# A two-layer graph network: the last h1 tiles, their Gram products and the channel statistics move ahead of the query heads

## The reference, cut to what matters

```
h   = relu(layernorm(x1))                       # "h1", 49 tiles of 128 rows
xn  = batchnorm(h)                              # mean and variance of each channel over all rows
agg = segment_sum(xn[src], dst) / max(deg, 1)   # 100,000 gathered rows
conv = relu(agg @ W_conv + b_conv)
# attention over the first 256 rows only (the batch is all zero, so one block of MAXN = 256)
qf, kf = phi(q, True), phi(k, False)            # random features, 256 of them, 8 heads of 64
attn = (qf @ (kf^T v)) / (qf @ sum(kf)) @ Wo
out = x1 + batchnorm(conv + attn + h)
```

## Time and profile before

| what | value |
|---|---|
| median of three runs | 3003.85 us |
| span of the profiled execution | 3541.0 us |
| the profiled execution's own time outside the span | not given by the page |
| mean granted TensorE clock | 0.883 of full speed |
| busy share: PE, PEld, DVE, ACT, POOL | 76%, 47%, 61%, 28%, 52% |
| gathers: first layer, second layer | 880, 784 |
| HBM traffic | 533.43 MB read, 54.10 MB written |

### The profile page before, as it was taken

One profiled execution on the slowest core, in us unless ns is written; L12 is line 12 of the kernel. 1 busy time (PEld: TensorE's weight loads), 2 busy tenths in 40 slices (PEclk: granted clock), 3 DMA queues, 4 the chain that ended last, 5 costly groups with the idle time before them and its releaser, 6 DMA issues. The chain is left out here.

```text
span 3541.0 us, 46052 instructions
## 1 busy us (share of the span) xinstructions
PE 2699.5 (76%) x10647; PEld 1671.1 (47%) x10692; DVE 2161.8 (61%) x3783; ACT 995.2 (28%) x3078; POOL 1858.0 (52%) x1883
## 2 busy tenths in 40 slices
PE   6887377777777877777777787877778788788991
PEld 4554256666656656655656652323333333233440
DVE  9999966666666767666668743333333333334668
ACT  6733334444443444434444520000000000000220
POOL 0000255555555556555555446666666666664667
PEclk8998678898988899898898897888889999999995
DMA  5110366666666666666665856666666666565226
GB/s 184 47 40 31 111 180 185 186 189 185 180 182 188 180 191 189 183 192 176 177 189 191 288 152 174 176 180 178 178 176 178 173 173 175 171 174 157 67 66 251
DMA packets 243449, 588.25 MB, mean 166 GB/s; under 512 B 57744, under 2 KB 82832, under 8 KB 243400
## 3 DMA queue, kind: packets, MB, share of 16 engines
q0 software_dynamic: 133120, 443.52, 43.8%
q1 hardware_dynamic: 110280, 144.14, 12.4%
HBM read 533.43 MB, written 54.10 MB: 166 GB/s over the span
## 5 line engine op out<-in xcount | busy, mean ns | idle before, releaser
L506 POOL DMA_INDIRECT big<-feat_table,idx x880 | 841.3, 956 | 1020.8 <-ACT idx L531 407.5
L1133 POOL DMA_INDIRECT big<-h_table,idx x784 | 743.6, 948 | 460.6 <-issue 235.2
L801 PE MATMUL psA<-big,onehot 128*128 128x260 f32 x1760 | 504.0, 436 | 120.1 <-DVE big L683 95.4
L801 PE MATMUL psB<-big,onehot 128*128 128x260 f32 x1760 | 479.8, 420 | 18.6 <-DVE acc L693 13.1
L801 PEld LDWEIGHTS psA<-big,onehot 128*128 128x128 f32 x1760 | 365.4, 216 | 208.3 <-issue 115.2
L557 ACT ACTIVATE big<-big,late_weights 128x65 f32<-128x65 f32 x1760 | 434.4, 343 | 0.0
L801 PEld LDWEIGHTS psB<-big,onehot 128*128 128x128 f32 x1760 | 351.5, 209 | 84.9 <-DVE acc L693 22.2
L531 ACT CAST idx<-minorB 128x8 int32 (+1 forms) x101 | 20.4, 204 | 1142.6 <-DMA big<-h_table,idx 1142.6
L1565 DVE TENSOR_TENSOR acc<-acc,psCD 128x512 f32 x176 | 120.7, 686 | 320.1 <-remote 106.2
L1565 DVE TENSOR_TENSOR acc<-acc,psA 128x512 f32 x176 | 120.7, 686 | 273.6 <-remote 103.3
L1859 PE MATMUL psA<-big,onehot 128*128 x352 | 199.3, 650 | 58.9 <-issue 42.7
(11 more groups left out here) (447 smaller groups left out, 3960.8 us busy)
## 6 DMA issues: line engine op xcount, KB each, us to landing
nodes_all<-slot_nodes SPq DMA_DIRECT2D x56, 512.0 KB
big<-feat_table,idx POOLq DMA_INDIRECT x880
feat_table<-big SPq DMA_DIRECT2D x49, 264.0 KB, 2.1
x_table<-acc SPq DMA_DIRECT2D x49, 256.0 KB, 3.8
h_table<-big SPq DMA_DIRECT2D x49, 256.0 KB, 4.0
big<-h_table,idx POOLq DMA_INDIRECT x784
big<-h_table SPq DMA_DIRECT2D x49, 256.0 KB, 2.6
big<-x_table SPq DMA_DIRECT2D x49, 256.0 KB, 4.3
```

The lines of the kernel that those rows point to most:

```text
L506: g.indirect_dma_start(ring[:, b.k, q * SB + u, :], None, feat_table, bass.IndirectOffsetOnAxis(ap=idx[:, 2 * b.k + q, u:u + 1], axis=0)). ...
L801: ins = pet.matmul(psum[:, 512 * hf:512 * hf + HALF_W], onehot[:, q, u % SB, :], ring[:, b.k, u, HALF_W * hf:HALF_W * (hf + 1)], start=(u ...
L1133: g.indirect_dma_start(big[:, place:place + D], None, h1_table, bass.IndirectOffsetOnAxis(ap=idx[:, r.c % CHUNK_CYCLE, b:b + 1], axis=0)). ...
```

## The change

Nothing is computed differently; four engine programs get another order. No instruction is added or taken away.

- ScalarE: tiles 38 to 48 of h1 are made in one run behind the last square root. The head loop holds the copy and the exponential alone.
- VectorE: `shift_q(0)` and the sixth key copy go ahead of the last x1 slot; the wait for all Gram products and the nine instructions of the statistics go ahead of the head loop, so that everything of the loop, `shift_q(1)` first, stands behind that wait.
- TensorE: two Gram products stand ahead of each of the first five key sums as before, one ahead of each of the last three (34, 35, 36). Then 37, the transposes of head 0, 38, 39, the features of head 2, 40 to 48, and then the head loop without Gram products.
- SyncE and GpSimd keep their text; what they wait for comes at other times.

```
--- before.py
+++ after.py
@@ layer1_scalar
-            for t in range(36, 40):
+            for t in range(36, 38):
                 h1_tile(t)
             deviations(7)
+            for t in range(38, TILES):
+                h1_tile(t)
             for h in hs:
                 SPE.wait(act, f"qfT{h}")
                 done(s.copy(qfT[...], psC[...]), f"qfT{h}")
                 if h < H - 2:
                     exp_q(h + 2)
-                h1_tile(40 + h)
-            h1_tile(TILES - 1)
@@ layer1_vector
             for h in range(KV_EARLY):
                 x1_upto((43, 45, 47, 49, 51)[h])
                 keep_kv(h)
+            shift_q(0)
+            keep_kv(KV_EARLY)
             x1_upto(TILES + 3)
-            shift_q(0)
-            for h in range(KV_EARLY, H):
+            for h in range(KV_EARLY + 1, H):
                 keep_kv(h)
...
-            for h in hs:
-                ... (shift_q(h + 1), max_q(h + 2), the division of head h)
             dve.wait_ge(grams, TILES)
             step(...)  # the nine instructions of the statistics
             assert k[0] == VAR_STEP
+            for h in hs:
+                ... (shift_q(h + 1), max_q(h + 2), the division of head h)
             step(v.memset(ones_mat, 1.0), False)
@@ layer1_tensor
-            for h in hs:
+            for h in range(KV_EARLY):
                 gram(24 + 2 * h)
                 gram(25 + 2 * h)
+                sum_kv(h)
+            for h in range(KV_EARLY, H):
+                gram(29 + h)
                 sum_kv(h)
...
+            gram(37)
             turn_q(0)
+            gram(38)
+            gram(39)
+            SACT.wait(pe, "eq0")
+            features(qT, 2, "uq")
+            for t in range(40, TILES):
+                gram(t)
             for h in hs:
-                if h < H - 2:
+                if 0 < h < H - 2:
                     SACT.wait(pe, f"eq{h}")
                     features(qT, h + 2, "uq")
...
                 if h < H - 1:
                     turn_q(h + 1)
-                if h >= 1:
-                    gram(39 + h)
-            gram(TILES - 2)
-            gram(TILES - 1)
```

More of the change, by code:

```diff
@@ L1489, in step @@
                     dve.wait_ge(bn1_step, k[0])
-            for h in hs:
-                if h < H - 1:
-                    shift_q(h + 1)
-                if h < H - 2:
[L1495 to L1504, removed]
             dve.wait_ge(grams, TILES)
@@ L1519, in layer1_vector @@
             assert k[0] == VAR_STEP
+            for h in hs:
+                if h < H - 1:
+                    shift_q(h + 1)
+                if h < H - 2:
+                    max_q(h + 2)
+                SPE.wait(dve, f"at{h}")
+                av = psE[:, h % 2 * 256:h % 2 * 256 + NT * (DH + 1)].rearrange("p (t d) -> p t d", t=NT)
+                z = zden[:, 2 * (h % 2):2 * (h % 2) + 2]
+                done(v.tensor_scalar(z, av[:, :, DH], KEPS, None, ALU.add), f"zd{h}")
+                SDVE.wait(dve, f"zd{h}")
+                done(v.reciprocal(z, z), f"zr{h}")
+                SDVE.wait(dve, f"zr{h}")
+                done(v.tensor_tensor(attn[:, :, h * DH:(h + 1) * DH], av[:, :, 0:DH],
+                                     z.unsqueeze(2).broadcast_to([P, NT, DH]), ALU.mult), f"at{h}")
             step(v.memset(ones_mat, 1.0), False)
```

## The result

| kernel | median, us | runs | ratio to the kernel before, 95% interval |
|---|---|---|---|
| before | 3003.01 | 15 | |
| changed | 3008.45 | 15 | 1.0019, 1.0011 to 1.0026 |

The change makes the kernel slower by 0.19%, 5.4 us. Forecast were 2988 us and a gain of 16; the time lies outside the range of 2978 to 3004 us.

The account below looks back on a forecast made before the run. GpSimd's gathers were taken to bound the row stage. The 25th gather 19 us earlier cut the profiled span from 3541 to 3522 us; scaled to the timed runs, 16 us gave 2988 us, range 2978 to 3004.

Parts of the forecast that it names:

- The last Gram product: TensorE ahead of the heads: the last Gram product comes at 2044.6 us, with 2044 and 2049 as ends.
- the seventh key sum: TensorE ahead of the heads: the seventh key sum loses its 4.87 us wait, as VectorE's shift avoids GpSimd's memset.
- the first gather: GpSimd, start of the row stage: gathers start at 2047 instead of 2070.41, 23.4 us earlier.
- The heads: Head loop: starts 4.0 us late, period falls from 3.43 to 2.44 us, transposes L1825 about 1.8 us earlier.
- the slower one: Rival: gathers beside the heads stall the engines, heads end 31 us later, 3014 us; chance 0.12.
- Port waits: VectorE's six later shifts beside gathers: 0.6 us of waiting in all, 5.7 us as the other end.
- The first release: SyncE's first freeing of ring space: the 25th gather goes at 2086 instead of 2105.20, 19 us earlier.
- its second rule: Instruction fetch: a taken branch out of the window forces a DMA fetch, so stalls belong to loops, not heads; outside the sum.
- The stage's pace: Row stage: both orders run at 11.7 us a row, so all behind it ends 19 us earlier.
- The rival in which TensorE paces the rows: Row stage of the timed runs: TensorE sets the pace, not gathers; gain 0 to 11 us, 2998 us; chance 0.22.
- the one in which a head start changes nothing: Rival, row stage: its even pace absorbs the head start, only 1.8 us remain, 3002 us; chance 0.08.

Follow-up runs that it names:

- e1: The changed kernel with the wait for all Gram products and the statistics put back behind VectorE's heads: 2991.46 us, ratio 0.9963 to the kernel before.
- e5: The changed kernel with 12 useless TensorE matmuls ahead of head 1's transposes and none in the head loop: 2997.52 us, ratio 0.9965 to the kernel before.
- second profile: The kernel before, unedited, run and profiled once more: median 3002.76 us, ratio 1.0000, span of the trace 3002.7 us.
- e2: The changed kernel with 4 useless TensorE matmuls behind each head's transposes and 12 ahead of head 1's: 2997.09 us, ratio 0.9981 to the kernel before.
- e6: e1 with three useless TensorE matmuls behind each of the last four heads and two more behind the last: 2997.64 us, ratio 0.9965 to the kernel before.
- e3: The kernel before with GpSimd's second memset repeated ahead of its first gather: 3006.90 us, ratio 1.0011 to the kernel before.
- e4: The kernel before with 24 useless TensorE matmuls ahead of the transposes of the attention output: 3002.18 us, ratio 1.0003 to the kernel before.
- e7: e6 with VectorE's last accumulator memset moved into its wait for the batch norm's shift row: 2991.37 us, ratio 0.9948 to the kernel before.

## Why the prediction was wrong

- *The last Gram product, the seventh key sum, the first gather.* Right. The shift took 0.42 us and the stall of 4.87 us at the key sums is gone (one of 1.80 us is left). The last Gram product ended 34.2 us behind the first memset, forecast 35.7, and the first gather followed 1.0 us behind it in place of 2.4, so it came 26 us earlier and not 23.4:

```profile
1684.41 0.42 DVE L1395 TENSOR_SCALAR onehot<-onehot 128x512 f32<-128x512 f32 x1
```

- *The heads.* This is the step that failed: "Then the loop is faster: its period of 3.43 us loses the Gram product's 0.99 us, 2.44 us, if TensorE stays its bound." The path of dependences was right (2.53 us in e1 and e5), but I priced it at full clock. The wait of 2.4 us for the statistics that I put ahead of it left TensorE idle for 2.33 us, and only the loop's short steps followed. The clock went to half and the period to 4.76 us. The transposes L1825 (L1832 in the changed kernel) came at 68.7, where the kernel before has them at 59.2 and the forecast was about 2 us ahead of that. Rows started at 85.6, 12.6 us late, in place of 1.8 us early. No term of the sum and no rival had the clock in it. Of the rivals the slower one had this place, but another mechanism: no wait on "remote" is seen beside the gathers.
- *Port waits.* Right at the lower end. The seven shifts beside gathers took 0.41 to 0.47 us in the changed kernel; in e1 five of them took 0.52 to 0.66, 0.9 us over 0.42 together, and the period stayed 2.53 us. The rule that the prediction weighed, of the Trainium skill ("SBUF — State Buffer", Who interferes with whom), by which one of the two engines blocks for the whole of the other's instruction, agrees in part: each of the five ended 0.25 us behind the end of a gather, but none was held for longer than 0.25 us, and a gather takes 0.95 us. A gather and the shift beside it, e1:

```profile
1711.38 0.95 POOL L1133 DMA_INDIRECT big<-h_table,idx  x1 [0.30 <-issue]
1711.92 0.66 DVE L1395 TENSOR_SCALAR onehot<-onehot 128x512 f32<-128x512 f32 x1
```

- *The first release.* The form was right, since the release followed the rows, but its size came from a trace that was not typical. I took 19 us from a 25th gather that waited 4.58 us for SyncE and from VectorE's 7.42 us stall; in the second profile neither exists (0.30 us and 1.1 us). So the stalls at the heads of loops, which the prediction took as agreeing with its second rule, are no support for it. In the second profile the gathers of the kernel before are unbroken, and where the ring is the limit the 33rd goes about 19.3 us behind the row start (18.4 to 20.2 in e1, e2, e5 and e6). With rows at 72, a little under 73.0, that is 91.3 in place of 101.6: the order could give about 10 us, which e1 gives (11.1 by its ratio, 8.9 in its trace), and not 16. So this term of the sum was mis-sized too. It is also the 33rd and not the 25th that decides, because the second row waits for VectorE's one-hot matrices, which stand behind its first add.
- *The stage's pace.* 11.7 us a row was of that trace alone. The pace is 10.0 us a row, GpSimd's issue and nothing else, in every other profile. The rival in which TensorE paces the rows falls with e3 and e4, and the one in which a head start changes nothing falls with e1; the 0.30 us between gathers is no artefact of profiling, since it stands in a trace of 3002.7 us.
- *Which warning I passed over.* The trace was 18% longer than the median (537 of 3004 us) and no view said where. I used it as a scale (0.85) and should have doubted the rows with "remote" as releaser first.

The accounting: rows 12.6 us later, of which the 9 us of slack that they had (33rd gather at 101.6, rows at 73.0 and about 19.3 from row to 33rd gather) absorb the most: 85.6 + 19.3 = 104.9, 3.3 us late. The ratio's interval says 3.3 to 7.8 us. The 2 us between the trace and the middle of it are not explained. The tail of the changed kernel's trace is 2.6 us longer than that of the kernel before, within what tails differ by.

## What to carry to other kernels

When filler work is moved out of a latency-bound loop on TensorE, price the loop at both clock levels, and look for the gap that the move opens ahead of it: 2.33 us of idleness, with a loop of short steps behind it, put the next 37.5 us at half speed here. A head start for a ring-limited producer is worth at most the ring, and only if the first release comes forward too; look at which gather waits for it in an undisturbed trace. A profile that is 18% longer than the runs it stands for has to be taken again before its waits are believed.

## What the runs showed of the hardware

- The clock did not come back while the loop itself ran, although TensorE counted as busy for 15.87 of 18.00 us there: the granted clock stayed 0.50 for the whole stretch. It came back within the 128x512 products behind. Before the idle 2.33 us the engine had been busy without a pause for 19.7 us.
- A gap by itself decides little. Behind 1.80 us of idle time ahead of a key sum in the changed kernel the clock stayed 1.00; behind 2.56 us at the same place in e1 it was 0.50 for 3.4 us, with Gram products following without a pause; behind 2.33 us with the head loop following it was 0.50 for 37.5 us.
- At the end of the heads, where TensorE idles 0.84 and 0.68 us (e5) or 0.85 and 0.68 us (e1) ahead of the last two products with the key sums and 0.78 us ahead of the last transposes, the clock fell behind the first of these in e5 and behind the second in e1. The last transposes took 1.97 us against 1.04 and the product with Wo 9.9 (e1) and 10.2 us (e5) against 7.1. With 14 useless matmuls there (e6, e7) it took 7.13 us.
- VectorE's shift and GpSimd's gathers hold each other, for a quarter of a microsecond at most. Thirteen shifts, in e1, e6 and e7, started 0.53 to 0.68 us into a gather; all took 0.52 to 0.67 us in place of 0.42 and ended 0.25 us behind the gather's end. Shifts that started 0.05 to 0.50 us into one took 0.41 to 0.43 us. Where a shift started 0.07 to 0.15 us ahead of a gather (the changed kernel, e2, e5), the gather took 1.10 to 1.17 us in place of 0.95.
- Beside GpSimd's memset the shift took 5.18 us again in the second profile of the kernel before, and ended 0.3 us behind the memset's end; 1.75 to 1.87 us in e1, e6 and e7, where it started later beside the memset.
